# Transposing and spreading the key norms over the whole array: zero-padded parts, 128 columns and 128 contraction rows

## The chip, the cores and the metric

The kernel runs on one core of one Trainium2 chip. The metric is the device time of one execution in microseconds. A core has a matrix engine (TensorE: PE for its matmuls, PEld for the loads of its stationary operand), VectorE (DVE), ScalarE (ACT), GpSimd (POOL) and a queue that issues DMAs (SP). Matmuls write to PSUM, here eight banks of 128 x 512 f32.

## What is computed

An input of 16 batches x 256 tokens x 128 channels passes an adaptive-layernorm attention block (once) and then a six-layer transformer block with windowed attention. The change touches the six layers. The part of the reference that matters:

```python
def l2norm(t):
    return t / jnp.maximum(jnp.linalg.norm(t, axis=-1, keepdims=True), 1e-12)

def attn_layer(x, Wqkv, qs, ksc, Wo):          # x: batch, 256 tokens, 128
    q, k, v = jnp.split(x @ Wqkv, 3, -1)       # 16 heads of 64 each
    q, k, v = (sh(q), sh(k), sh(v))
    q = l2norm(q) * qs
    k = l2norm(k) * ksc
    ...                                        # rotary tables on q and k
    out = local_attention(q, k, v)             # windows of 32, keys of two windows
    return out @ Wo

for i in range(DEPTH):                         # 6
    x = attn_layer(shift_tokens(x), ...) + x
    x = ffn_layer(shift_tokens(x), ...) + x
```

The norms of k are one number for each token and head, so a key tile (partitions = channels, columns = tokens) has to be multiplied by a row that differs from head to head.

## The kernel before, in words

After a first phase (the attention block, some 180 us) the kernel walks through 6 x 16 = 96 "batches" of a layer, one batch a period. Every engine has a hand-written order of steps for one period (PE_ORDER, DVE_ORDER, ACT_ORDER, POOL_ORDER, SP_ORDER), in which steps of neighbouring batches are interleaved; each engine runs its list strictly in order and waits on semaphores for the others. So a step that comes late on an engine holds up all that stands behind it there.

The steps around the change, in the order of PE: PA and PB project queries and keys (L1229); NK and NQ sum the squares of a head (L1240, 32 output partitions each); TK and TQ transpose the norms (L1248, f32). ACT makes the reciprocal norms rk of the keys out of them (RTK). POOL splits rk into three bf16 parts, that is high, middle and rest, in four instructions (RK, the last of them L591). TU (L1255) transposes them: for each half of the tokens the 128 x 48 bf16 tile rk_bf (3 parts x 16 heads) is the stationary operand of a matmul with the bf16 identity, so the result has 48 partitions. DVE copies it to rkt (UC, L997). KN0 and KN1 (L1264) spread the norms: the stationary operand is a selection matrix head_sel_bf of 48 x 128, the moving one rkt of 48 x 256, and contracting over the 48 rows adds the three parts up and repeats each head's norm over that head's channels. DVE multiplies the keys by the result (KM0, KM1, L1004), two instructions each, and writes them to ks.

What stands between on PE: `T00 TU NQ KN0 PAD V1 PV00 KN1 TQ T01 V2 DN T10`. V1 and V2 (L1274) project values, T00, T01 and T10 transpose probabilities (L1303), PV00 multiplies probabilities and values in 64 x 64 blocks (L1321), DN is the down projection of the feed-forward layer (L1367, its last part with 85 rows). Scores (L1292) run in 64 x 32 blocks.

PSUM: PA, PB, TU, KN, V, T and DN take turns on a ring of three banks (bank_of, bank_free); a step waits until the bank's last user was read. DN has KN1's bank, so it waits for KM1; V3 has V2's bank, which ACT copies out (VC2, L731). KM1 also starts the DMAs of the keys (SP's MK). On DVE the order is `UC H2 KM0 CQ VC1 KM1 AR10 TC01`, on POOL `AN00 AD3 TB RK AN01`, where AD adds the rotary products (L612) and AN scales probabilities (L597).

Of the kernel before, what the change touches and what calls it, by code (L numbers as in the profile page):

```python
# [8 lines left out]
BF16 = mybir.dt.bfloat16  # L9
# [4 lines left out]
P = 128  # L14
BATCH, TOKENS, DIM = 16, 256, 128
DEPTH, HEADS, DIM_HEAD, WINDOW = 6, 16, 64, 32
# [4 lines left out]
TILES = TOKENS // P  # L21
# [6 lines left out]
HALF = DIM_HEAD // 2  # L28
QUADS = HEADS // 4
COUPLES = QUADS // 2  # L30
QK_BANKS = 4 * COUPLES
MOVES = 8
V_MOVES = 16
V_STEPS = 2 * TILES
PARTS = 4
# [83 lines left out]
def build(nc, t):  # L119

    with ExitStack() as ctx:
        def sb(name, shape, dt=F32):
            return ctx.enter_context(nc.sbuf_tensor(name, shape, dt))
# [14 lines left out]
        ident_bf = sb("ident_bf", [P, P], BF16)  # L138
        mask_bf = sb("mask_bf", [P, TILES, PAIRS, KEYS], BF16)
        head_ones = sb("head_ones", [P, WINDOW])  # L140
        head_sel_bf = sb("head_sel_bf", [3 * HEADS, QUADS, P], BF16)
        rotary = sb("rotary", [P, 2, 2, TOKENS])
        mean_ones = sb("mean_ones", [P, P])
        center = sb("center", [P, P])
# [26 lines left out]
        log_norm2 = sb("log_norm2", [P, 2, TILES, HEADS])  # L171
        rk = sb("rk", [P, TILES, HEADS])
        rk_rest = sb("rk_rest", [P, TILES, HEADS])
        rk_bf = sb("rk_bf", [P, TILES, 3, HEADS], BF16)
        rkt = sb("rkt", [3 * HEADS, TOKENS], BF16)
        qt = sb("qt", [P, PAIRS, TOKENS])
        kt = sb("kt", [P, PAIRS, PADDED])
        vs = sb("vs", [P, TILES, 2, PAIRS * DIM_HEAD])
# [31 lines left out]
        def carve(parts, *shape):  # L210
            size = int(np.prod(shape))
            room = PAIRS * TOKENS
            if carved[0] % room + size > room:
                carved[0] = -(-carved[0] // room) * room
            at_ = carved[0] % room
            v2_ = v2[0:parts, :, :].rearrange("p w n -> p (w n)")
            prod_ = prod[0:parts, :, :, :, :].rearrange("p i a f c -> p (i a f c)")
            rooms = (prod_[:, 0:room], prod_[:, room:2 * room], v2_[:, 0:room], v2_[:, room:2 * room],
                     qt[0:parts, :, :].rearrange("p j c -> p (j c)"),
                     att_t[0:parts, :, :].rearrange("p j c -> p (j c)"),  # L220
                     vs[0:parts, :, :, :].rearrange("p t e n -> p (t e n)"))
            view = rooms[carved[0] // room][:, at_:at_ + size]
            carved[0] += size
            if len(shape) == 2:
                return view.rearrange("p (a b) -> p a b", b=shape[1])
            if len(shape) == 3:
                return view.rearrange("p (a b c) -> p a b c", b=shape[1], c=shape[2])
            return view
# [50 lines left out]

        mod_a = carve(P, BATCH, 6)  # L280
        mask = carve(P, TILES, KEYS)
        head_sel = carve(3 * HEADS, QUADS, P)
        wmod = carve(P, 6 * DIM)


# [48 lines left out]
        def at(g, per_batch, n=0):  # L334

            return g * per_batch + (CREDIT + n)
# [4 lines left out]

        def moved(g, n=0, moves=MOVES):

            return (g + n) * (16 * moves)
# [57 lines left out]
        def bank_of(s):  # L402

            return ring_ps[RING.index(s) % BANKS]
# [123 lines left out]
        def _(pool):  # L528
# [2 lines left out]
            pool.memset(xs1[:, :], 0.0)  # L531
            pool.memset(mean_ones[:, :], 1.0 / DIM)
            pool.memset(ones_bf[:, :], 1.0)
            pool.memset(kt[:, :, 0:WINDOW], 0.0).then_inc(memset_done, 1)

            def make_tables(layer):
# [82 lines left out]
        def _(act):  # L619
# [98 lines left out]
            def step(s, g, b, parity, layer):  # L718
# [8 lines left out]
                if kind == "VC":  # L727
                    act.wait_ge(v_made, at(g, V_STEPS, rank(PE_ORDER, ("V", s[1]), "V") + 1))
                    if s[1] == 0 and g > 0:
                        act.wait_ge(v_moved, moved(g, 0, V_MOVES))  # L730
                    nc.scalar.activation(vs[:, s[1] // 2, 0, :], bank_of(("V", s[1]))[:, :], ACT.Copy  # L731
# [74 lines left out]
        def _(dve):  # L806
# [161 lines left out]
            def step(s, g, b, parity, layer):  # L968
# [24 lines left out]
                if kind == "UC":  # L993
                    dve.wait_ge(rk_turned, at(g, 1, 1))
                    dve.wait_ge(kn_made, at(g, COUPLES))
                    turn = bank_of(("TU",))[0:3 * HEADS, 0:TOKENS // 2].bitcast(BF16)
                    V.tensor_copy(rkt[:, :], turn).then_inc(rkt_ready, 1)  # L997
                if kind == "KM":
                    c = s[1]
# [6 lines left out]
                if kind == "VC":  # L1006
                    dve.wait_ge(v_made, at(g, V_STEPS, rank(PE_ORDER, ("V", s[1]), "V") + 1))
                    if s[1] == 1 and g > 0:
                        dve.wait_ge(v_moved, moved(g, 0, V_MOVES))
                    V.tensor_copy(vs[:, s[1] // 2, 1, :], bank_of(("V", s[1]))[:, :]).then_inc(v_odd_ready, 1)  # L1010
# [63 lines left out]
                if kind == "X":  # L1074
                    dve.wait_ge(w2_ready, at(g, 1, 1))
                    V.scalar_tensor_tensor(out=x_all[:, columns(b)], in0=bank_of(("DN",))[:, 0:TOKENS], scalar=vecs[layer % 2][:, 2:3],
                                           in1=x1[:, :], op0=ALU.add, op1=ALU.add).then_inc(x_ready, 1)

            walk(DVE_ORDER, step)
            for b in range(BATCH):  # L1080
                dve.wait_ge(e_turned, at(b, 1, 1))
# [6 lines left out]
        def _(pe):  # L1088
# [111 lines left out]
            def bank_free(g, s):  # L1200

                u, gu = user_before(RING, s, g, BANKS)
                if u is None:
                    return
                if u[0] in ("PA", "PB"):
                    pe.wait_ge(sq_ready, at(gu, QK_BANKS, rank(ACT_ORDER, ("Q" + u[0][1], u[1]), "QA", "QB") + 1))
                if u[0] == "TU":
                    pe.wait_ge(rkt_ready, at(gu, 1, 1))
                if u[0] == "KN":
                    pe.wait_ge(kn_ready, at(gu, COUPLES, u[1] + 1))  # L1210
                if u[0] == "V":
                    pe.wait_ge(v_odd_ready if u[1] % 2 else v_even_ready, at(gu, TILES, u[1] // 2 + 1))
                if u[0] == "T":
                    pe.wait_ge(t_copied, at(gu, 2 * TILES, 2 * u[1] + u[2] + 1))
                if u[0] == "DN":
                    pe.wait_ge(x_ready, at(gu, 1, 1))

            def step(s, g, b, parity, layer):
# [31 lines left out]
                if kind == "TU":  # L1250
                    pe.wait_ge(rk_parts, at(g, 4, 4))
                    bank_free(g, s)
                    turn = bank_of(s)[0:3 * HEADS, 0:TOKENS // 2].bitcast(BF16)
                    for i in range(TILES):
                        last = pe.transpose(turn[:, P * i:P * (i + 1)],  # L1255
                                            rk_bf[:, i, :, :].rearrange("p a h -> p (a h)"), ident_bf[:, :])
                    last.then_inc(rk_turned, 1)
# [48 lines left out]
                if kind == "PV":  # L1306
                    i, c = s[1], s[2]
                    if (i, c) == (0, 0):
                        pe.wait_ge(hidden_ready, at(g, FCHUNKS))
                        pe.wait_ge(v_moved, moved(g, 1, V_MOVES))  # L1310
                        if g == 0:
# [51 lines left out]
                if kind == "DN":  # L1363
# [5 lines left out]
                    last.then_inc(w2_ready, 1)  # L1369

            walk(PE_ORDER, step)
            for b in range(BATCH):
                pe.wait_ge(e_fin, at(b, 1, 1))
# [10 lines left out]
def shape_constants():  # L1384

    half = np.arange(0, DIM_HEAD, 2, dtype=np.float32)
    inv_freq = (np.float32(1.0) / np.float32(10000.0) ** (half / np.float32(DIM_HEAD))).astype(np.float32)
    pos = np.arange(TOKENS, dtype=np.float32)
    freqs = (pos[:, None] * inv_freq[None, :]).astype(np.float32).astype(np.float64)
    base = ((half + np.float32(0.4 * DIM_HEAD)) / np.float32(1.4 * DIM_HEAD)).astype(np.float64)  # L1390
    scale = base[None, :] ** ((pos - TOKENS // 2) / (WINDOW // 2)).astype(np.float64)[:, None]
    four = []
    for s in (1.0 / scale, scale):
        cos, sin = np.cos(freqs) * s, np.sin(freqs) * s
        four += [np.concatenate([cos] * 4, 1), np.concatenate([sin] * 4, 1)]
    rotary = np.stack([f.T for f in four], 1).astype(np.float32).reshape(P, 2, 2, TOKENS)
    query = np.arange(P)[:, None] % WINDOW
    key = np.arange(KEYS)[None, :]
    hidden = (key > query + WINDOW) | (query > key)
    mask = np.zeros((P, TILES, KEYS), np.float32)  # L1400
    for i in range(TILES):
        no_window = (i == 0) & (np.arange(P)[:, None] < WINDOW) & (key < WINDOW)
        mask[:, i] = np.where(hidden | no_window, MASKED, 0.0)
    head_ones = np.zeros((P, WINDOW), np.float32)
    head_sel = np.zeros((HEADS, QUADS, P), np.float32)
    for r in range(4):
        head_ones[HALF * r:HALF * (r + 1), r] = 1.0
        for u in range(QUADS):
            head_sel[4 * u + r, u, HALF * r:HALF * (r + 1)] = 1.0
    return {"ident": np.eye(P, dtype=np.float32), "mask": mask, "head_ones": head_ones,  # L1410
            "head_sel": np.concatenate([head_sel] * 3), "rotary": rotary,
            "biases": np.tile(np.array([LN_EPS, 0.0], np.float32), (P, 1)),
            "ones_row": np.ones((1, P), np.float32)}

# [37 lines left out]
```

## Time and profile before

| what | value |
|---|---|
| device time, median of 3 runs | 3501.78 us (3486.22 to 3502.32) |
| span of the profiled execution | 3500.8 us, what lies around the span is not shown |
| PE busy | 3344.2 us (96%) |
| PEld busy | 2479.3 us (71%) |
| DVE busy | 2441.7 us (70%) |
| ACT busy | 2702.7 us (77%) |
| POOL busy | 1445.3 us (41%) |
| TU's matmuls (L1255) | 192, mean 233 ns |
| KN's matmuls (L1264) | 384, mean 281 ns |

Matmuls overlap in the pipeline, so the mean duration of one is longer than the distance from one to the next; to price a step, the distance between the ends of steps is read. In the chain of waits each piece begins where the one before ends, so there the pieces are these distances.

### The profile page before, as it was taken

Reading aid. Unit: us, or ns where it says so; the run is one execution under the profiler, and the core shown is the slowest. Engines: PE = TensorE matmul, PEld = TensorE weight load, DVE = VectorE, ACT = ScalarE, POOL = GpSimd, SP = SyncE. Lnnn points to the kernel's source line nnn. Section 1 sums busy time; section 2 is a strip of 40 time slices with the busy share of each in tenths; the row PEclk is TensorE's granted clock in tenths of the full one; section 3 lists DMA queues with packets and bytes.
Section 4 is the critical chain, followed back from the end, with each engine's and each line's share of the span. In section 5 each row is a group of like instructions: output and inputs, shape, how many; then the busy total and the mean of one; then the engine's idle time right before and its main releaser. Section 6 shows DMA issues by size and latency. Waiting matters only on the chain.

```text
span 3500.8 us, 152322 instructions
## 1 busy us (share of the span) xinstructions
PE 3344.2 (96%) x63036; PEld 2479.3 (71%) x63228; DVE 2441.7 (70%) x5141; ACT 2702.7 (77%) x9033; POOL 1445.3 (41%) x1276
## 2 busy tenths in 40 slices
PE   6789999999999999999999999999999999999997
PEld 4457777677777767777767777767767767777775
DVE  5667777667777767777767777767767767777774
ACT  5667787768778777878777887868778787878876
POOL 2244444434444443444444444444444353444441
PEclk9899999999999999999999999999999999999998
DMA  2055656555655656565565566555555655565563
GB/s 71 1 115 122 140 122 129 121 123 120 143 123 123 132 118 134 127 130 126 112 138 118 127 135 131 120 130 117 127 129 121 133 129 127 117 130 126 116 135 76
DMA packets 361273, 421.42 MB, mean 120 GB/s; under 512 B 52291, under 2 KB 265814, under 8 KB 359814
## 3 DMA queue, kind: packets, MB, share of 16 engines
q1 hardware_dynamic: 360582, 411.67, 54.4%
q8 instruction: 499, 8.18, 1.0%
q14 instruction: 192, 1.57, 0.1%
HBM read 19.30 MB, written 2.10 MB: 6 GB/s over the span
## 4 chain that ended last, share of the span: by engine, by line
PE 69%; POOL 18%; issue 4%; DVE 2%; DMA 1%; ACT 1%; SPq 0%; POOLq 0%; DVEq 0%
PE ring_ps L1229 16%; POOL qs L612 12%; PE out_ps L1321 12%; PE out_ps L1331 9%; PE ring_ps L1274 8%; PE small_ps L1240 6%; PE score_ps L1292 4%; PE ring_ps L1303 4%; PE ring_ps L1367 4%; POOL probs L597 3%; DVE prod L988 2%; PE ring_ps L1264 2%; PE out_ps L1345 2%; PE score_ps L1284 1%; PE small_ps L1248 1%
## 5 line engine op out<-in xcount | busy, mean ns | idle before, releaser
L769 ACT ACTIVATE probs<-score_ps,neg_max,rq 128x64 f32<-128x64 f32 x3072 | 1194.7, 420 | 97.0 <-DVE neg_max L1026 95.7
L988 DVE TENSOR_TENSOR prod<-ring_ps,tables 128x512 f32<-128x512 f32 x1536 | 957.9, 681 | 292.4 <-PE ring_ps L1229 264.8
L612 POOL TENSOR_TENSOR ks<-prod 128x1024 f32<-128x1024 f32 x192 | 452.9, 2359 | 870.9 <-DVE prod L988 870.9
L1229 PE MATMUL ring_ps<-xs,wqk 128*128 128x256 f32 x3072 | 771.2, 389 | 17.2 <-issue 11.9
L769 ACT ACTIVATION_READ_ACCUMULATOR probs<-score_ps,neg_max,rq 128x1 f32 x3072 | 677.4, 221 | 0.0
L725 ACT ACTIVATE square<-ring_ps,biases 128x512 f32<-128x512 f32 x768 | 516.9, 687 | 200.9 <-DVE prod L988 199.1
L597 POOL TENSOR_TENSOR probs<-probs,inv_sums 128x512 f32<-128x512 f32 x384 | 401.0, 1044 | 608.8 <-DVE inv_sums L1040 608.7
L1229 PEld LDWEIGHTS ring_ps<-xs,wqk 128*128 128x128 f32 x3072 | 572.9, 192 | 107.3 <-issue 18.9
L612 POOL TENSOR_TENSOR qs<-prod 128x1024 f32<-128x1024 f32 x192 | 453.4, 2361 | 395.1 <-DVE prod L988 395.1
L1321 PEld LDWEIGHTS out_ps<-pt,v 64*64 64x64 f32 x24576 | 399.5, 136 | 119.2 <-issue 117.0
L758 ACT ACTIVATE att_t<-out_ps 128x512 f32<-128x512 f32 x384 | 217.0, 591 | 312.1 <-PE out_ps L1321 311.5
L1321 PE MATMUL out_ps<-pt,v 64*64 64x32 f32 x24576 | 433.4, 221 | 9.5 <-issue 6.7
L1274 PE MATMUL ring_ps<-wv,xs 128*128 128x512 f32 x768 | 431.1, 644 | 0.7 <-ACT vs L731 0.7
L1331 PE MATMUL out_ps<-att_t,wo 128*128 128x256 f32 x1536 | 350.9, 381 | 1.9 <-ACT att_t L758 1.2
L1292 PEld LDWEIGHTS score_ps<-kt,qt 64*32 64x32 f32 x24576 | 264.5, 105 | 90.2 <-issue 82.4
L1331 PEld LDWEIGHTS out_ps<-att_t,wo 128*128 128x128 f32 x1536 | 292.5, 191 | 43.5 <-issue 2.2
L1033 DVE COPY pt<-ring_ps 128x512 f32<-128x512 f32 x384 | 259.6, 676 | 82.2 <-PE out_ps L1321 78.2
L1292 PE MATMUL score_ps<-kt,qt 64*32 64x64 f32 x24576 | 297.8, 226 | 6.1 <-issue 5.0
L1004 DVE TENSOR_TENSOR ks<-ks,ring_ps 128x512 f32<-128x512 f32 x384 | 246.7, 684 | 73.0 <-PE ring_ps L1264 72.6
L1360 PE MATMUL out_ps<-xg,w 128*128 128x256 f32 (+1 forms) x1152 | 283.8, 383 | 3.2 <-DVE xg L1064 3.2
L1021 DVE TENSOR_REDUCE row_max<-score_ps 128x8 f32<-128x512 f32 x384 | 246.4, 684 | 24.1 <-PE score_ps L1292 20.2
L1360 PEld LDWEIGHTS out_ps<-xg,w 128*128 128x128 f32 (+1 forms) x1152 | 199.3, 180 | 80.6 <-DVE hidden L1071 30.2
(182 smaller groups left out, 3809.4 us busy)
## 6 DMA issues: line engine op xcount, KB each, us to landing
v<-vs SPq DMA_DIRECT2D x1344, 128.0 KB
qt<-qs SPq DMA_DIRECT2D x768, 128.0 KB
kt<-ks SPq DMA_DIRECT2D x768, 128.0 KB
v<-vs SPq DMA_DIRECT2D x192, 64.0 KB
wqk<-in_L_ffn_Wqkv SPq DMA_DIRECT2D x6, 1024.0 KB, 5.2
wv<-in_L_ffn_Wqkv SPq DMA_DIRECT2D x6, 512.0 KB, 4.5
wo<-in_L_ffn_Wo SPq DMA_DIRECT2D x6, 512.0 KB
out_dram<-ks SPq DMA_DIRECT2D x16, 128.0 KB, 1.9
```

The lines of the kernel that those rows point to most:

```text
L597: pool.tensor_tensor(probs[i][:, part, :, :].rearrange("p j e k -> p (j e) k"), probs[i][:, part, :, :].rearrange("p j e k -> p (j e) k"), ...
L612: pool.tensor_tensor(dst, prod_a[p % 2], prod_b[p % 2], ALU.add).then_inc(rot_ready, 1)
L725: nc.scalar.activation(square[p % COUPLES][a][:, :], bank_of(("PB" if a else "PA", p))[:, :], ACT.Square, bias=zero_col[:, :]).then_inc(sq ...
L769: last = nc.scalar.activation(probs[i][:, j, e, :], score_ps[e][:, KEYS * j:KEYS * (j + 1)], ACT.Exp, bias=neg_max[:, h:h + 1], scale=rq[p ...
L988: last = V.tensor_tensor((prod_b if a else prod_a)[p % 2][:, f, :] .rearrange("p (u c) -> p u c", u=2), bank[:, :].rearrange("p (u c) -> p ...
L1033: V.tensor_copy(pt[:, 4 * c:4 * c + 4, :], bank_of(("T", i, c))[:, :].rearrange("p (j c) -> p j c", c=P)).then_inc(t_copied, 1)
L1229: last = mm(bank_of(s)[:, TOKENS * f:TOKENS * (f + 1)], wqk[:, n, 2 * c + f, a, :], xs[:, WINDOW:PADDED], start=True, stop=True)
L1274: mm(bank_of(s)[:, :], xs[:, WINDOW + P * i:WINDOW + P * (i + 1)], heads[:, :, e, :], start=True, stop=True).then_inc(v_made, 1)
L1292: last = mm(score_ps[e][WINDOW * w:WINDOW * (w + 1), KEYS * j:KEYS * (j + 1)], qt[64 * e:64 * e + 64, j, q0:q0 + WINDOW], kt[64 * e:64 * e ...
L1321: last = mm(out_ps[j % 2][side:side + 64, q0:q0 + WINDOW], v2[64 * e:64 * e + 64, WPT * i + w, DIM_HEAD * j:DIM_HEAD * (j + 1)], pt[64 * e ...
L1331: last = mm(out_ps[0][:, 0:TOKENS], wo[layer % 2][:, j, :], att_t[:, j, :], start=(j == 0), stop=(j == PAIRS - 1))
L1360: last = mm(out_ps[c % 2][0:size, TOKENS * n:TOKENS * (n + 1)], w1[layer % 2][:, col:col + size], xg[:, :], start=True, stop=True)
```

## The change

rk_bf gets eight parts of 16 heads in place of three; parts 3 to 7 are set to zero once, on POOL at the start, and never written again. So TU's stationary operand is 128 x 128 and its result has 128 partitions. rkt and the selection matrix get 128 rows; the rows of the matrix that belong to the padding are zero. UC copies 128 partitions, KN contracts over 128 rows. Numbers of instructions, their order and the waits in the loop stay as they are. The f32 constant head_sel that is loaded once grows from 48 to 128 rows of 2 KB.

```diff
+RK_PARTS = P // HEADS
-        head_sel_bf = sb("head_sel_bf", [3 * HEADS, QUADS, P], BF16)
+        head_sel_bf = sb("head_sel_bf", [P, QUADS, P], BF16)
-        rk_bf = sb("rk_bf", [P, TILES, 3, HEADS], BF16)
-        rkt = sb("rkt", [3 * HEADS, TOKENS], BF16)
+        rk_bf = sb("rk_bf", [P, TILES, RK_PARTS, HEADS], BF16)
+        rkt = sb("rkt", [P, TOKENS], BF16)
-        head_sel = carve(3 * HEADS, QUADS, P)
+        head_sel = carve(P, QUADS, P)
...
             pool.memset(ones_bf[:, :], 1.0)
+            pool.memset(rk_bf[:, :, :, :], 0.0)
             pool.memset(kt[:, :, 0:WINDOW], 0.0).then_inc(memset_done, 1)
...
                 if kind == "UC":
...
-                    turn = bank_of(("TU",))[0:3 * HEADS, 0:TOKENS // 2].bitcast(BF16)
+                    turn = bank_of(("TU",))[:, 0:TOKENS // 2].bitcast(BF16)
                     V.tensor_copy(rkt[:, :], turn).then_inc(rkt_ready, 1)
...
                 if kind == "TU":
                     pe.wait_ge(rk_parts, at(g, 4, 4))
                     bank_free(g, s)
-                    turn = bank_of(s)[0:3 * HEADS, 0:TOKENS // 2].bitcast(BF16)
+                    turn = bank_of(s)[:, 0:TOKENS // 2].bitcast(BF16)
...
-    head_sel = np.zeros((HEADS, QUADS, P), np.float32)
+    head_sel = np.zeros((RK_PARTS, HEADS, QUADS, P), np.float32)
...
-            head_sel[4 * u + r, u, HALF * r:HALF * (r + 1)] = 1.0
+            head_sel[0:3, 4 * u + r, u, HALF * r:HALF * (r + 1)] = 1.0
...
-            "head_sel": np.concatenate([head_sel] * 3), "rotary": rotary,
+            "head_sel": head_sel.reshape(P, QUADS, P), "rotary": rotary,
```

## Rows read from the trace of the kernel before

**Rows 1.** The page: span, and busy time of the engines.
```profile
span 3500.8 us, 152322 instructions
PE 3344.2 (96%) x63036; PEld 2479.3 (71%) x63228; DVE 2441.7 (70%) x5141; ACT 2702.7 (77%) x9033; POOL 1445.3 (41%) x1276
```

**Rows 2.** Chain of waits, 2029 to 2064 us: start us, us, what.
```profile
2029.05 0.26 POOL rk_bf L591
...
2029.34 0.29 PE ring_ps L1255 x2
...
2030.64 0.32 PE ring_ps L1264 x2
2030.96 1.06 PE ring_ps L1274 x2
...
2033.40 0.37 PE small_ps L1248 x2
...
2034.21 0.86 PE ring_ps L1274 x2
2035.07 1.30 PE ring_ps L1367 x6
...
2037.87 1.05 PE ring_ps L1274 x2
...
2047.21 3.45 PE out_ps L1331 x16
...
2052.53 0.63 PE out_ps L1345 x2
```

**Rows 3.** Timeline of PE, 2018 to 2024 us: TK after a projection.
```profile
2021.26 1.89 PE L1229 MATMUL ring_ps<-xs,wqk 128*128 128x256 f32 x8
2022.98 0.38 PE L1248 MATMUL small_ps<-ident,norm 128*128 128x128 f32 x2
```

**Rows 4.** All waits: who waited for whom, us in total, times, longest.
```profile
PEld ring_ps L1255 <- POOL rk_bf L591: 65.0, 96, 6.5
PEld ring_ps L1367 <- DVE ks L1004: 49.5, 92, 0.5
PE ring_ps L1229 <- issue: 11.9, 12, 1.5
```

**Rows 5.** Loads of the stationary operand by form: rows*columns, count, busy us, mean ns.
```profile
L1360 PEld LDWEIGHTS out_ps<-xg,w 128*128 128x128 f32 x768 | 140.4, 193 | 19.7 <-DVE xg L1064 4.1
L1360 PEld LDWEIGHTS out_ps<-xg,w 128*85 128x85 f32 x384 | 58.9, 154 | 60.9 <-DVE hidden L1071 30.2 <-issue 18.7
L1284 PEld LDWEIGHTS score_ps<-mask_bf,ident_bf 128*128 128x128 bf16 x384 | 37.5, 98 | 28.0 <-ACT probs L769 0.4 <-issue 0.3
L1264 PEld LDWEIGHTS ring_ps<-rkt,head_sel_bf 48*128 48x128 bf16 x384 | 21.4, 95 | 47.3 <-DVE rkt L997 35.8 <-issue 6.1 <-DVE ks L1004 1.5
L1255 PEld LDWEIGHTS ring_ps<-ident_bf,rk_bf 128*48 128x48 bf16 x192 | 12.1, 102 | 65.0 <-POOL rk_bf L591 65.0
```

**Rows 6.** Timeline, 2033.3 to 2038 us: KM1, DN, VC2 and V3.
```profile
2033.44 1.28 DVE L1004 TENSOR_TENSOR ks<-ks,ring_ps 128x512 f32<-128x512 f32 x2 [0.23 <-PE ring_ps L1264]
...
2034.78 1.18 PEld L1367 LDWEIGHTS ring_ps<-hidden,w 128*128 128x128 f32 x6 [0.54 <-DVE ks L1004]
...
2034.90 1.46 PE L1367 MATMUL ring_ps<-hidden,w 128*128 128x256 f32 x6
...
2036.81 0.65 ACT L731 ACTIVATE vs<-ring_ps 128x512 f32<-128x512 f32 x1
...
2037.80 0.30 PEld L1274 LDWEIGHTS ring_ps<-wv,xs 128*128 128x128 f32 x2
```

**Rows 7.** Timeline, 2107 to 2110 us: a gap on PE in the projections.
```profile
2108.99 1.35 PE L1229 MATMUL ring_ps<-xs,wqk 128*128 128x256 f32 x5 [0.93 <-issue]
```

**Rows 8.** Timeline, 0 to 60 us: POOL's first work on constants and on a batch.
```profile
13.79 0.30 POOL L549 CAST ident_bf<-ident 128x128 bf16<-128x128 f32 x1 [11.55 <-DMA rotary<-const_rotary]
...
36.75 0.41 POOL L564 TENSOR_TENSOR prod<-v,qt 128x128 f32<-128x128 f32 x1 [16.27 <-ACT qt L675]
```

## The prediction

> **What bounds the kernel now.** I read the page first: PE is busy for 96% of the span [rows 1]. Then the chain of waits over one period of some 33 us, because a busy PE may still be waiting in effect. The chain stays on PE from TU to the last projections, piece after piece without a gap, and returns to PE through POOL's rotary sums and the split of rk, whose last instruction ends 0.03 us before TU begins [rows 2]. The waits say the same: TU's load waited for that instruction 96 times of 96 [rows 4]. So between TU and the projections PE alone sets the pace, and what is saved there shortens the period if nothing else becomes late; TU's start hangs on POOL.
>
> Next I price each step of PE by its piece in the chain, and look for equal work at unequal prices. Two matmuls of 128x512 f32 take 0.86 us after a transpose (L1274 at 2034.21), but 1.06 us after KN0 and 1.05 us after the 64*64 blocks of L1321 [rows 2]. Two f32 transposes of norms take 0.37 us after KN1 [rows 2]; behind a projection they end 23.36 - 23.15 = 0.21 us after it (end of one row to end of the other) [rows 3], say 0.22. Sixteen matmuls of L1331 take 3.45 us, 0.216 us each, so DN's six at 1.30 us have no surcharge, though its last ones have 85 rows; L1345's two would be 0.43 us and take 0.63 us after a step with 32 columns [rows 2]. So surcharges of 0.15 to 0.20 us stand where PE passes from small blocks to a full operand, and a step of 48 rows counts as small, one of 85 doesn't.
>
> The Trainium skill, "TensorEngine Tiling (Array Packing)", Key Properties, has the rule for it: changing the tiling mode drains the engine. By that rule a 48-row step is a change of mode on the way in and out; the trace agrees, with 0.20 us on the way out to a 128-column f32 load and 0.15 us to a transpose.
>
> **KN0 and V1.** Removed: the way out of KN0. V1 should cost 0.86 in place of 1.06 us: -0.20 us a period. The way into KN0 stays, since NQ has 32 columns: 0.32 us now [rows 2], of which two bf16 matmuls of 256 columns at half of f32's 0.216 us are 0.22, the entry 0.10. No row shows a 128-row bf16 operand entered from small blocks. Bounds: unchanged (its load of 98 ns at L1284 is like KN's 95 [rows 5]) or the entry of L1345, 0.63 - 0.43 = 0.20, so +0.10. I take unchanged, because the bf16 loads are alike and L1345's is f32.
>
> **KN1 and TQ.** The way in from PV00 stays, with the same bounds of 0 to +0.10. The way out to TQ goes: 0.37 to 0.22, -0.15 us.
>
> **TU.** The two loads grow from 48 to 128 columns. T00 before it has full operands, NQ behind has 32 columns, so the way in would go and the way out stays. But the way in is hidden: the load waits for POOL in all 96 periods [rows 4]; nothing is gained there. The larger load: 98 ns at L1284 against 102 ns now [rows 5], no more. In f32, 85 columns take 154 and 128 take 193 ns [rows 5], 0.9 ns a column; at that price 80 columns more are +0.07 us on the first load, which stands bare, and some +0.03 us on the second, half hidden. Bounds -0.03 (the pair at full pace) and +0.10; I take 0, by the bf16 row.
>
> The Trainium skill, "TensorE: Matmul & The Clock Gate", LDWEIGHTS, speaks against the change: a load's time is its columns over 1.2. By it 80 columns cost 67 ns a load, an estimate. The trace's bf16 rows don't agree (128 columns 95 and 98 ns, 48 columns 102); its f32 rows do.
>
> **UC, KM, POOL, DMA.** UC copies as many columns on more partitions; KN0 waits for PE's own NQ, not for UC. The instructions, waits and DMAs of the loop are the same. The memset and 160 KB more of constants come once, in 11.55 us in which POOL waits for constants and before 16.27 us in which it waits again [rows 8]; without that cover they would cost 1 to 2 us, once.
>
> **What is late next.** DN must wait until KM1 has read KN1's bank. Its load waited for KM1 92 times [rows 4]: KM1 ends at 34.72, the load starts at 34.78, DN at 34.90 [rows 6]. An f32 load keeps its matmul back some 0.10 us (L1345's entry against KN's), so DN could start at 34.88: 0.02 us of slack. KM1 follows KN1 directly (DVE had idled 0.23 us for it [rows 6]). So the 0.20 us saved ahead of KN1 moves KM1 and passes whole, and DVE's idle 0.23 us just covers it. The 0.15 us saved at TQ, behind KN1, is stopped: PE would be at DN 0.15 us sooner, KM1 would not. Only 0.02 us of it passes. A second gate lies behind: V3 needs VC2, which ends at 37.46, and V3's load starts at 37.80 [rows 6]; with 0.05 us for the signal it can come 0.29 us sooner. 0.22 us fits, all 0.35 would not.
>
> **Sum.** 0.20 + 0.02 = 0.22 us a period; 96 periods: 21 us. 3500.8 - 21 = 3480 us by the profiled execution; its span is 1 us from the median of the runs, 3501.8, so 3480 stands for the median too. The runs shown differ by 16 us; a measurement of this kernel tells some 0.5% (17.5 us) from no change, and 21 is barely above.
>
> **Rivals.**
> (a) KM1 isn't the gate, for instance because KN's result is read sooner. Then V3's 0.29 us caps it: -28 us, 3473. For it: the slack of 0.02 is a difference of small numbers. Against: 92 waits.
> (b) The entries into the full bf16 operand cost as in f32: 0.22 - 2 x 0.10 = 0.02 us, -2 us, 3499. For it: no row shows this entry. Against: like loads.
> (c) Loads go by columns: TU costs 0.10 us more, 0.22 - 0.10 = 0.12 us, -12 us, 3489. For it: f32 rows. Against: bf16 rows.
> (d) The change doesn't do what it says: the surcharge behind KN comes from the passage from bf16 to f32, which stays. 0 us, 3501. Against: L1274 has the same surcharge behind f32 blocks of L1321.
> (e) Slower: PE runs out of instructions. In some periods it stands in the projections with nothing to wait for, once for 0.93 us [rows 7]; this happened 12 times at L1229, for 11.9 us in all [rows 4]. If a shorter period has PE catch up with its supply more often, each case costs about 1 us, a period's gain nearly five times over: 21 more cases eat the gain, 39 make it 18 us slower, 3519. Against: it is rare, and the steps before it wait for others.
>
> **How the numbers follow.** Forecast 0.60, (a) 0.08, (b) 0.10, (c) 0.09, (d) 0.06, (e) 0.07. The likeliest is 3480, its own range 3472 to 3488. The range takes in (a), (b) and (c) and leaves out (d) in part and (e): 3466 to 3500. Faster by over 0.5%: 0.9 of the forecast's 0.60 and (a), 0.62. Slower: (e), 0.07. Within 0.5%: 0.31.
>
> **What would show it.** Right: V1's piece behind KN0 at 0.86, TQ's behind KN1 at 0.22, KN at 0.32, DN's step longer by 0.13 us with its load waiting for KM1, TU still started by POOL, the median period shorter by 0.22 us. (a): no such lengthening at DN, but V3 waiting for ACT. (b): KN at 0.42. (c): TU's load near 170 ns. (d): V1 still 1.06. (e): more idle "issue" at L1229. The prediction is wrong if a 128-row operand has a surcharge that no row shows, or if the clock granted to PE falls when more of the array is fed.

## The result and the profile after

| what | before | changed |
|---|---|---|
| median of five runs | 3489.75 us | 3467.4 us (3462.67 to 3475.43) |
| ratio, changed to before | | 0.9926, 95% interval 0.9909 to 0.9943 |
| span of the profiled execution | 3500.8 us | 3469.5 us (time 3471.32) |

The changed kernel is faster by 0.74% (0.57 to 0.91%), some 26 us; run again later against 17 runs of before it was 0.992 (0.9898 to 0.9941), 28 us. The forecast was 0.6%, or 3480 us; 3467.4 us lies below its own range of 3472 to 3488 us and just inside the wide one of 3466 to 3500. All ratios here are of executions in the usual state: of the twelve of tu_only, one took 12064 us at a granted clock of 0.259 and is left out of its ratio.

The page of the changed kernel; compare [rows 1]:

```profile
span 3469.5 us, 152515 instructions
PE 3320.9 (96%) x63228; PEld 2474.7 (71%) x63228; DVE 2440.1 (70%) x5141; ACT 2702.4 (78%) x9033; POOL 1445.5 (42%) x1277
```

PE is still busy for 96%, and no engine has another share of note. The difference is in PE's steps. The chain of waits of the changed kernel over a part of one period, from the end of RK to V3, with start, length and step (its lines stand two lower than before's: L1257 is TU, L1266 KN, L1276 V, L1250 TK and TQ, L1369 DN); compare [rows 2]:

```profile
2009.20 0.25 POOL rk_bf L593
...
2009.50 0.28 PE ring_ps L1257 x2
2009.79 1.00 PE small_ps L1242 x16
2010.79 0.32 PE ring_ps L1266 x2
2011.11 0.86 PE ring_ps L1276 x2
2011.97 1.06 PE out_ps L1323 x64
2013.04 0.33 PE ring_ps L1266 x2
2013.36 0.22 PE small_ps L1250 x2
...
2014.02 0.86 PE ring_ps L1276 x2
2014.88 1.42 PE ring_ps L1369 x6
...
2017.81 1.05 PE ring_ps L1276 x2
```

V1 behind KN0 takes 0.86 where it took 1.06 us, and TQ behind KN1 0.22 where it took 0.37. KN's own pair is as long as it was. V3, whose step before it is still in 64*64 blocks, still pays: 1.05. DN has become longer, 1.42 in place of 1.30. This period is not a lucky pick: the medians over all periods, of the distance from the end of one step to the end of the next, went from 1.06 to 0.86 us for V1, from 0.37 to 0.22 for TQ and from 1.30 to 1.43 for DN, and PV00, T01, V2 and T10 are as before. The period from TU to TU has a median of 33.01 us instead of 33.27, and a lower quartile of 32.84 instead of 33.06. Why DN is longer, its load shows, in the timeline and in all waits of the changed kernel; compare [rows 6] and [rows 4]:

```profile
2012.68 0.68 DVE L1012 COPY vs<-ring_ps 128x512 f32<-128x512 f32 x1
...
2013.40 1.28 DVE L1006 TENSOR_TENSOR ks<-ks,ring_ps 128x512 f32<-128x512 f32 x2
...
2014.73 1.16 PEld L1369 LDWEIGHTS ring_ps<-hidden,w 128*128 128x128 f32 x6 [0.69 <-DVE ks L1006]
2014.74 1.56 PE L1369 MATMUL ring_ps<-hidden,w 128*128 128x256 f32 x6
```

```profile
PEld ring_ps L1369 <- DVE ks L1006: 64.7, 94, 0.7
DVE ks L1006 <- PE ring_ps L1266: 50.8, 99, 2.1
PEld ring_ps L1257 <- POOL rk_bf L593: 64.2, 96, 6.6
PE ring_ps L1231 <- issue: 10.0, 12, 1.3
```

KM1 ends at 14.68, DN's load starts 0.05 us later (0.06 before), but DN now stands directly behind it instead of 0.12 us after it, and DVE no longer idles ahead of KM1. TU waits for POOL 96 times, as before.

The second of these rows holds a limit that the change has just reached. In the kernel before it read:

```profile
DVE ks L1004 <- PE ring_ps L1264: 72.6, 188, 2.1
```

That was KM0 and KM1 of nearly every period; what is left is mostly KM0. The median idle time ahead of KM1 fell from 0.225 to 0.034 us. KM1 now starts right behind DVE's own copy of V1 (VC1, L1012), so whatever else were saved ahead of KN1, KM1 and with it DN's bank could come hardly any sooner. No run here tries that.

Loads of the stationary operand of the changed kernel; compare [rows 5]:

```profile
L1266 PEld LDWEIGHTS ring_ps<-rkt,head_sel_bf 128*128 128x128 bf16 x384 | 21.9, 97 | 47.1 <-DVE rkt L999 36.6 <-issue 5.3 <-DVE ks L1006 1.2
L1257 PEld LDWEIGHTS ring_ps<-ident_bf,rk_bf 128*128 128x128 bf16 x192 | 11.0, 98 | 64.2 <-POOL rk_bf L593 64.2
```

KN's went from 95 to 97 ns, TU's from 102 to 98, with 128 columns in place of 48.

### The profile page after: what moved, and what is told of

It reads as the page before. It is cut to its first block, busy times and chain, and to the rows that moved or that the text cites. A ratio compares the mean times of both kernels' runs of the same rounds, so it can differ in the third digit from the quotient of the medians.

```text
span 3469.5 us, 152515 instructions
## 1 busy us (share of the span) xinstructions
PE 3320.9 (96%) x63228; PEld 2474.7 (71%) x63228; DVE 2440.1 (70%) x5141; ACT 2702.4 (78%) x9033; POOL 1445.5 (42%) x1277
## 4 chain that ended last, share of the span: by engine, by line
PE 69%; POOL 17%; issue 4%; DVE 2%; DMA 1%; SPq 1%; ACT 0%; POOLq 0%; DVEq 0%
PE ring_ps L1231 16%; POOL qs L614 12%; PE out_ps L1323 12%; PE out_ps L1333 10%; PE ring_ps L1276 8%; PE small_ps L1242 6%; PE score_ps L1294 5%; PE ring_ps L1369 4%; PE ring_ps L1305 4%; POOL probs L599 3%; DVE prod L990 2%; PE ring_ps L1266 2%; PE out_ps L1347 2%; PE score_ps L1286 1%; PE ring_ps L1257 1%
## 5 line engine op out<-in xcount | busy, mean ns | idle before, releaser
L1231 PE MATMUL ring_ps<-xs,wqk 128*128 128x256 f32 x3072 | 771.8, 389 | 14.8 <-issue 10.0
L1231 PEld LDWEIGHTS ring_ps<-xs,wqk 128*128 128x128 f32 x3072 | 573.3, 192 | 104.1 <-issue 17.1
L1323 PE MATMUL out_ps<-pt,v 64*64 64x32 f32 x24576 | 432.0, 221 | 12.8 <-issue 10.5
L1276 PE MATMUL ring_ps<-wv,xs 128*128 128x512 f32 x768 | 418.3, 627 | 1.0 <-ACT vs L733 0.7
```

Of the source, the lines that this page charges most:

```text
L1231: last = mm(bank_of(s)[:, TOKENS * f:TOKENS * (f + 1)], wqk[:, n, 2 * c + f, a, :], xs[:, WINDOW:PADDED], start=True, stop=True)
L1276: mm(bank_of(s)[:, :], xs[:, WINDOW + P * i:WINDOW + P * (i + 1)], heads[:, :, e, :], start=True, stop=True).then_inc(v_made, 1)
L1323: last = mm(out_ps[j % 2][side:side + 64, q0:q0 + WINDOW], v2[64 * e:64 * e + 64, WPT * i + w, DIM_HEAD * j:DIM_HEAD * (j + 1)], pt[64 * e ...
```

## The experiments

The theory at the start: PE pays 0.15 to 0.20 us when it passes from small blocks to full operands; KN counts as small with 48 rows; KM1 stops what is saved behind KN1. Rivals: TU gives part of the gain; loads go by their columns; the surcharge goes with the type or with the number of rows. All ratios are to runs of the kernel before on the same chip, with the 95% interval; "..." in a diff stands for lines left out.

### KN alone and TU alone

```diff
 # kn_only, against the changed kernel
-        rk_bf = sb("rk_bf", [P, TILES, RK_PARTS, HEADS], BF16)
+        rk_bf = sb("rk_bf", [P, TILES, 3, HEADS], BF16)
...
-            pool.memset(rk_bf[:, :, :, :], 0.0)
+            pool.memset(rkt[:, :], 0.0)
... # in UC; the view turn has 48 partitions again, in UC and in TU
-                    V.tensor_copy(rkt[:, :], turn).then_inc(rkt_ready, 1)
+                    V.tensor_copy(rkt[0:3 * HEADS, :], turn).then_inc(rkt_ready, 1)
```

> Only KN contracts over 128 rows; TU keeps its 48 columns, and rows 48 to 127 of rkt are zeroed once. Theory (passages between small blocks and full operands, KM1 as the gate at DN): the whole gain of the change, because TU's way in hides behind POOL: V1 behind KN0 0.86 us, TQ behind KN1 0.22, DN 1.43, 20 to 27 us less than before, within 3 us of the changed kernel. Rival (TU's full operand gives part of the gain, as the 5 us that the runs show over my sum might hint): V1 and TQ the same, but TU and NQ behind it longer than in the changed kernel by 0.05 us or more, 5 us or more lost.

Measured: 0.9922 (0.9906 to 0.9938). Its chain of waits, behind KN0 and KN1:

```profile
2008.34 0.29 PE ring_ps L1257 x2
2009.96 0.86 PE ring_ps L1276 x2
2012.21 0.22 PE small_ps L1250 x2
2013.72 1.43 PE ring_ps L1369 x6
```

```diff
 # tu_only, against the kernel before
-        rk_bf = sb("rk_bf", [P, TILES, 3, HEADS], BF16)
+        rk_bf = sb("rk_bf", [P, TILES, RK_PARTS, HEADS], BF16)
...
+            pool.memset(rk_bf[:, :, :, :], 0.0)
... # in TU
-                    turn = bank_of(s)[0:3 * HEADS, 0:TOKENS // 2].bitcast(BF16)
+                    turn = bank_of(s)[:, 0:TOKENS // 2].bitcast(BF16)
```

> Only TU has 128 columns, KN contracts over 48 rows as before. Theory: no change, within 3 us of before; V1 behind KN0 1.06 us, TQ behind KN1 0.37, TU's pair 0.34. Rival (loads go by columns): TU's loads near 170 ns and the pair longer by 0.10 us, 10 us slower than before. Rival (TU's way in counts): 5 us or more faster than before.

Measured: 0.9987 (0.9973 to 1.0001), that is 0 to 9 us faster, 5 at the middle. Its chain:

```profile
2021.53 0.29 PE ring_ps L1257 x2
2023.14 1.05 PE ring_ps L1276 x2
2025.58 0.37 PE small_ps L1250 x2
2027.25 1.30 PE ring_ps L1369 x6
```

All steps are as before, TU's pair too (0.29 us; the 0.34 that was expected for it was too high), and its loads took 98 ns, not 170. So KN alone makes the gain, and TU's 128 columns neither cost the 10 us of the rule by columns nor give anything that a row of the period shows. The middle of the interval is at 5 us, just where my rival had put its mark. The steps speak against it, and kn_only, which lacks TU's columns, has lost nothing; a gain of a few us outside these steps isn't excluded.

### How many rows count as full

rows64 and rows80 have RK_PARTS = 4 and 5, and RK_PARTS * HEADS rows in rkt, head_sel and head_sel_bf:

```diff
-RK_PARTS = P // HEADS
+RK_PARTS = 4          # rows80: 5
+ROWS = RK_PARTS * HEADS
...
-        head_sel_bf = sb("head_sel_bf", [P, QUADS, P], BF16)
+        head_sel_bf = sb("head_sel_bf", [ROWS, QUADS, P], BF16)
...
-        rkt = sb("rkt", [P, TOKENS], BF16)
+        rkt = sb("rkt", [ROWS, TOKENS], BF16)
... # the same in the constants and in the views of UC and TU
```

> Four parts in place of eight: TU has 64 columns, KN contracts over 64 rows. Theory: 64 rows still run as a small block, so the surcharges of before stay: V1 1.06 us, TQ 0.37 us, DN 1.30 us, within 3 us of before. Rival (the surcharge comes from the passage from bf16 to f32, or from the number of rows in proportion): it would fall with the rows, or be gone as in the changed kernel: V1 between 0.86 and 1.03.

> Five parts: TU has 80 columns, KN contracts over 80 rows. Theory: above 64 rows an operand counts as full (L1367 with 85 rows paid nothing), so all of the gain is there: V1 0.86 us, TQ 0.22, DN 1.43, within 3 us of the changed kernel. Rival (in proportion to the rows, or only 128 rows count): V1 above 0.93 us and less than half of the gain.

Measured: rows64 0.9998 (0.9986 to 1.0009), rows80 0.9917 (0.9902 to 0.9932). The chain of rows64 (L1277 is V1, L1251 TQ, L1370 DN):

```profile
2005.51 1.05 PE ring_ps L1277 x2
2007.95 0.37 PE small_ps L1251 x2
2009.62 1.30 PE ring_ps L1370 x6
```

and of rows80:

```profile
2008.59 0.86 PE ring_ps L1277 x2
2010.84 0.22 PE small_ps L1251 x2
2012.35 1.43 PE ring_ps L1370 x6
```

With 64 rows nothing of the surcharge is gone, with 80 all of it, at the same type and the same instructions. That excludes the type and the number of rows in proportion. The loads of TU, first of rows64, then of rows80:

```profile
L1258 PEld LDWEIGHTS ring_ps<-ident_bf,rk_bf 128*64 128x64 bf16 x192 | 13.4, 110 | 64.8 <-POOL rk_bf L594 64.8
```

```profile
L1258 PEld LDWEIGHTS ring_ps<-ident_bf,rk_bf 128*80 128x80 bf16 x192 | 14.8, 117 | 64.2 <-POOL rk_bf L594 64.2
```

So bf16 loads do go by columns up to 80 (102, 110, 117 ns for 48, 64, 80), yet 128 columns take 98.

### Is KM1 the gate at DN

after_swap and before_swap exchange V2 and DN on PE. The bank that waits for KM1 then belongs to V2, which stands behind DN and so needs it 0.44 us later than DN did behind V2 (1.30 against 0.86 us).

```diff
-TQ T01 V2 DN T10 PV01 V3 T11 PV10 PV11
+TQ T01 DN V2 T10 PV01 V3 T11 PV10 PV11
```

> The changed kernel with DN moved ahead of V2 on PE (T01 DN V2 T10 in place of T01 V2 DN T10), so that the step with KN1's bank, which waits for KM1, is V2, 0.44 us later, and DN takes V1's bank. Theory (KM1 stops 0.13 us of TQ's gain at DN): the six matmuls of DN take 1.30 us again, V2's pair 0.86 without a wait for KM1, the period shrinks by up to another 0.13 us, 10 to 12 us less than the changed kernel; T10, which waits for POOL, has only some 0.1 us left and may keep 0.02 us of it. Rival (DN's 1.43 us is not a wait for KM1 but some cost of its own, or POOL's scaling stops it at T10): no more than 3 us less than the changed kernel.

> The same move in the kernel before. Theory: KM1 costs DN nothing there (slack 0.02 us), so nothing is gained: within 3 us of before, DN's six at 1.30 us. Rival (the move is good or bad by itself): 5 us or more away from before.

> The changed kernel itself, unchanged, beside the two with DN moved, so that they are compared on one chip. Every theory: 0.992 to 0.995 of before.

Measured: after_swap 0.9872 (0.9854 to 0.9891), median 3452.9 us; after_again 0.992 (0.9898 to 0.9941), 3470.5; before_swap 1.0002 (0.9987 to 1.0017). The chain of after_swap, and its wait for KM1:

```profile
2002.33 1.30 PE ring_ps L1369 x6
2003.63 0.86 PE ring_ps L1276 x2
2004.49 0.46 PE ring_ps L1305 x4
```

```profile
PEld ring_ps L1276 <- DVE ks L1006: 2.5, 2, 1.5
```

DN is back at 1.30 us, and the wait for KM1 is gone (2 times in place of 94). T10 (L1305) ends 0.02 us later than without the move, 0.46 against 0.44 us, as expected; its load waits for POOL. That makes 0.11 us a period, 10.5 us in all, and the lower quartile of the period fell by 0.11 us too. The medians of the runs differ by 17.6; both intervals are some 7 us wide to each side, and no run shows whether the other 7 us are more than this scatter. In the kernel before the same move gives nothing: its six of DN take 1.30 us with and without it. So the gate was not there before the change and was made by it. after_swap is the fastest kernel of the study, 1.3% below before.

### The part of the gain that the sum didn't have

The steps give 0.22 us a period, 21 us, as forecast. The runs give 26 to 28. I read the time from TU to TU in the two profiles. The 80 periods away from the changes of layer shrink from 2689.0 to 2672.5 us in all, 0.21 each. The 15 periods at the five changes of layer (the one that ends with the long wait and the two behind it) shrink from 549.9 to 538.0, 12 us in place of 3. The first difference is less firm than it looks: over all profiles, 80 such periods with the same steps scatter by 10 to 16 us. At a change of layer PE stands for some 6 us while POOL waits for the next layer's scales and builds its tables, and the granted clock falls from 2.4 to 1.2 GHz.

Windows of 4 us around one such change: length, then busy time of PE, PEld, DVE, ACT and POOL with the number of instructions, then the granted clock (1.00 is 2.4 GHz), the DMA share and GB/s. Of the kernel before:

```profile
688.00:692.00 4.00, 0.00 (x0) 0.00 (x0) 0.17 (x1) 3.99 (x18) 4.00 (x6) 1.00 0.97 204
692.00:696.00 4.00, 2.68 (x20) 0.88 (x20) 0.67 (x2) 3.06 (x16) 1.93 (x6) 0.50 0.20 38
696.00:700.00 4.00, 4.00 (x68) 2.37 (x68) 2.31 (x4) 0.00 (x0) 0.00 (x0) 0.50 0.01 4
700.00:704.00 4.00, 4.00 (x12) 2.47 (x13) 2.09 (x4) 0.25 (x1) 1.04 (x1) 0.50 0.18 35
704.00:708.00 4.00, 4.00 (x76) 3.13 (x75) 0.94 (x3) 0.77 (x2) 1.04 (x1) 0.80 0.94 195
```

and of the changed kernel:

```profile
684.00:688.00 4.00, 0.06 (x1) 0.06 (x2) 0.00 (x0) 4.00 (x22) 3.67 (x9) 0.58 0.85 176
688.00:692.00 4.00, 4.00 (x26) 1.38 (x26) 1.90 (x5) 1.77 (x10) 0.89 (x1) 0.56 0.00 0
692.00:696.00 4.00, 4.00 (x81) 3.12 (x80) 2.95 (x7) 0.60 (x1) 1.04 (x1) 1.00 0.02 4
```

Before: some 13.6 us at 1.2 GHz; changed: 3.4 + 3.5 = 6.9. My first guess was that the KN of a layer's first batch did it. Starting from kn_only (TU with 48 columns, rkt zeroed once), I gave that batch alone 128 rows:

```diff
 # kn_first, in KN; kn_rest has the two numbers exchanged
+                        rows = P if b == 0 else 3 * HEADS
-                        last = mm(bank_of(s)[...], head_sel_bf[:, 2 * c + f, :], rkt[:, :], start=True, stop=True)
+                        last = mm(bank_of(s)[...], head_sel_bf[0:rows, 2 * c + f, :], rkt[0:rows, :], start=True, stop=True)
```

> KN contracts over 128 rows only in the first batch of each layer (6 of 96), over 48 rows in the others; TU has 48 columns. That is the KN that runs at a change of layer, where the granted clock is at 1.2 GHz. Theory (the rest of the gain, 6 to 9 us over my 21, comes from PE getting 2.4 GHz back sooner at the changes of layer, and it is this KN that does it): the stretches at 1.2 GHz at the five changes of layer are 6.8 us each instead of 6.8 to 13.7, and the time is 6 to 10 us less than before. Rival (the stretches at a change of layer have to do with the steady periods ahead of it, or with chance): stretches as in before, about 1 us less than before.

> The counterpart: KN over 48 rows in the first batch of each layer, over 128 rows in the other 90. Theory: the stretches at 1.2 GHz at the changes of layer last 6.8 to 13.7 us as before, and the gain is that of the steady periods alone, 0.22 us x 90 = 20 us. Rival (the steady periods bring the clock back sooner): stretches of 6.8 us and the whole gain, 27 us.

Measured: kn_first 0.999 (0.9975 to 1.0005), kn_rest 0.9929 (0.9903 to 0.9954). The first stretch at 1.2 GHz at the five changes was 6.8, 13.7, 10.2, 10.2 and 6.8 us in kn_first, and at most 6.8 in kn_rest. In time, kn_rest kept some 25 us of the gain, nearer to the 27 of the rival than to the 20 of the theory, and kn_first brought 3.5 in place of 6 to 10: the theory as written fell. The timeline of the kernel before shows why. TU after the wait belongs to the last batch of the layer, the sixteenth, since POOL builds the tables (TB) between that batch's AD3 and RK, and TU waits 5.94 us:

```profile
693.32 0.41 PE L1255 MATMUL ring_ps<-ident_bf,rk_bf 128*48 128x128 bf16 x2 [5.94 <-POOL rk_bf L591]
```

kn_last and kn_not_last are the same pair with `b == BATCH - 1`.

> The runs before took the wrong batch: the KN that runs when the clock is at 1.2 GHz is that of the last batch of a layer, whose TU waits for POOL some 6 us while POOL builds the tables of the next layer. Here KN contracts over 128 rows only in that last batch (6 of 96, 5 of them ahead of a change of layer), TU with 48 columns. Theory (a KN over 128 rows right after the wait brings 2.4 GHz back sooner): stretches at 1.2 GHz of 6.8 us or less at all five changes of layer, 5 to 10 us less than before in all. Rival (the steady periods ahead decide, or chance): stretches up to 13.7 us as in before, 1 us less than before.

> The counterpart: KN over 48 rows in the last batch of each layer, over 128 rows in the other 90. Theory: stretches at 1.2 GHz of 6.8 to 13.7 us as in before, and only the gain of the steady periods, 0.22 us x 90 = 20 us. Rival: 6.8 us or less each, and the whole gain, 27 us.

Measured: kn_last 0.9979 (0.9967 to 0.9992), 7 us for a change in 6 of 96 batches; kn_not_last 0.9947 (0.9928 to 0.9967), 18.5 us. Windows of 30 us around the first three changes of layer of kn_last:

```profile
685.00:715.00 30.00, 24.07 (x593) 17.28 (x594) 16.79 (x35) 17.25 (x51) 14.66 (x18) 0.89 0.61 149
1232.00:1262.00 30.00, 23.80 (x587) 16.70 (x588) 15.31 (x32) 16.64 (x50) 13.71 (x18) 0.89 0.55 133
1776.00:1806.00 30.00, 24.02 (x590) 16.69 (x591) 16.29 (x33) 17.05 (x50) 14.63 (x18) 0.89 0.57 141
```

and of kn_not_last:

```profile
685.00:715.00 30.00, 24.08 (x469) 17.20 (x469) 15.55 (x32) 15.76 (x55) 12.48 (x17) 0.89 0.59 133
1228.00:1258.00 30.00, 23.59 (x453) 15.94 (x452) 13.35 (x28) 13.16 (x45) 10.48 (x16) 0.77 0.49 107
1774.00:1804.00 30.00, 24.16 (x462) 16.99 (x462) 15.58 (x33) 14.62 (x50) 11.69 (x16) 0.83 0.53 118
```

A mean of 0.89 in 30 us is 6.6 us at half clock, 0.83 is 10.2, 0.77 is 13.8. Over all profiles: in the seven kernels where this KN has 80 or 128 rows, none of the 35 first stretches is longer than 6.8 us (in kn_last and rows80 one was followed by 3.4 us more); in the six where it has 48 or 64, 21 of 30 are 10.2 or 13.7 us. Each of these is one profile. 7 and 18.5 us make 26, the gain of the whole change within its interval; of the 7, 1.3 are the 0.22 us that each of the six batches saves anyway, so the clock brings some 6 (2 to 10 by kn_last's interval). The 15 periods at the changes of layer agree: of the six kernels with 48 or 64 rows in a layer's last batch, they take 546.1 to 556.1 us (550.1 in kn_not_last); of the others, 544.0 in kn_last and 536.1 to 541.2 in the remaining six.

## Why the prediction was right or wrong

- **The surcharge and its place: right.** V1 1.06 to 0.86 and TQ 0.37 to 0.22, as read from [rows 2] and [rows 3]. That it hangs on the rows, and that 64 still count as small and 80 as full, rows64 and rows80 showed; the trace of before had only 48 and 85. Rival (d), the type, is excluded by them.
- **The way into KN: right.** 0.32 and 0.33 us with 128 rows. The upper bound of +0.10 us, which rested on an f32 load, was far off, and with it rival (b).
- **TU: right.** Its pair is 0.28 us in the changed kernel and 0.29 with 48 columns; POOL's RK starts it all 96 times. Rival (c), the load by columns, is out: 98 ns. It was a fair rival: with 80 columns the load is slower (117 ns) than with 48. By the rule of the Trainium skill, "TensorE: Matmul & The Clock Gate", LDWEIGHTS, that the prediction set beside it, 43 more columns cost 36 ns and a load of 128 columns takes 107 ns, both estimates. The f32 rows agree with the first alone, with 39 ns (154 to 193), and not with the second, with 193 ns; the prediction's "its f32 rows do" said too much.
- **KM1 as the next gate: right, and now shown.** DN grew by 0.12 to 0.13 us, the 0.13 of the forecast; without that gate (after_swap) it is back. Rival (a) is out. That DVE's idle 0.23 us just covered the 0.20 saved ahead of KN1 was right too: 0.03 are left.
- **Rival (e), instruction supply:** 12 times at L1231 for 10.0 us in the changed kernel, as in [rows 4]. It didn't move.
- **The sum: the step that failed is "96 periods: 21 us", one price for all.** The 0.22 us itself was right; a term was missing beside it. In the five periods at a change of layer the rows of the last batch's KN bear on how long PE stays at 1.2 GHz after its wait; what this gives is some 6 us (kn_last: 3 to 12 with the six batches' own 1.3), so that the runs gave 26 to 28 us in place of 21. The prediction put this term at nothing without a reason. I had named a fall of the granted clock as a danger and never asked whether the clock's low stretches could get shorter. The clock of the whole span, 0.982, looked as if there were nothing to gain; in 3500 us that is still some 125 us at half clock.
- **The level: the second step that failed is "so 3480 stands for the median too".** I anchored 3480 on the profiled execution and the median of the three runs shown, 3501.8. Over five runs beside the changed kernel the median of before was 3489.75, and in four later sets of runs 3490.8 to 3494.9. So of the 12.6 us between 3480 and 3467.4, the larger part, some 7 to 12, is where before's three runs had fallen; what is left is no more than the clock's term. As a difference, 21 us were forecast and 22 to 28 measured (22 between the two medians, 26 and 28 by the ratios).

## What to carry to other kernels

In the chain of waits, compare the pieces of equal steps behind different neighbours: a step that costs 0.2 us more behind one neighbour than behind another shows what the neighbour costs, and a matmul that contracts over 64 rows or fewer, ahead of a full one, may be cheaper with its contraction padded beyond 64 rows (80 did here). Behind every saving look for the first step whose wait ends within the saving; here it was KM1 with 0.02 us of slack, and moving one step past another gave back what it had stopped. Price the rare periods (a change of layer, a table, a late DMA) apart from the common ones, and read the granted clock there, not as a mean of the span.

## What the runs showed of the hardware

- PE passing out of a matmul of 48 or 64 rows into a full f32 operand cost 0.20 us, into an f32 transpose 0.15 us; out of one of 80, 85 or 128 rows nothing. A pair of bf16 matmuls entered from blocks of 64*64 or 128*32 took the same with 48 and with 128 rows, 0.32 and 0.33 us. The Trainium skill, "TensorEngine Tiling (Array Packing)", Key Properties, says that a change of mode drains the engine and gives no price; the trace agrees, and these are the prices here.
- A bf16 load took 102, 110 and 117 ns with 48, 64 and 80 columns and 98 with 128. The Trainium skill, "TensorE: Matmul & The Clock Gate", Weight-path perf modes, has a fast load for 128 columns that are not f32; by that rule 128 is the exception and the trace agrees. The 0.9 ns a column of the f32 rows do not hold for bf16: from 48 to 80 columns it was 0.5.
- After PE had stood some 6 us and its clock had fallen to 1.2 GHz, the stretch at 1.2 GHz lasted at most 6.8 us in 35 of 35 cases where the spreading matmuls that followed had 80 or 128 rows, and 10.2 or 13.7 us in 21 of 30 cases where they had 48 or 64. What in them does it (the rows, or the surcharge that goes with them) no run tells apart; this stays open.
